# A graph attention layer on one core: VectorE's order of work at a change of super-row

## The reference

```python
h = relu(layernorm(x))                                   # 8192 x 256
Wh = h @ W_w + W_b
e = leaky_relu((Wh @ a1)[:, None] + (Wh @ a2)[None, :])  # 8192 x 8192
attention = softmax(where(adj > 0, e, -9e15), axis=1)
out = x + attention @ Wh
```

## Time and profile before

| | |
|---|---|
| time, median of 3 runs | 1593.36 us (1593.07 to 1595.46) |
| time of the profiled execution | 1592.53 us |
| its span, first to last instruction | 1590.7 us |
| TensorE busy | 1464.8 us (92%) |
| VectorE busy | 1421.9 us (89%) |
| ScalarE busy | 1116.6 us (70%) |
| GpSimd busy | 592.6 us (37%) |
| the 16 DMA engines, mean use in a super-row | 0.72 to 0.75 |

### The profile page before, as it was taken

How to read it: one execution, slowest core, us unless ns; L and a number is a source line. 1 busy time by engine, 2 the same in 40 slices (tenths; PEclk the granted TensorE clock), 3 DMA queues, 4 the chain that set the end, 5 groups by cost and what they waited for, 6 DMA issues and landing times.

```text
span 1590.7 us, 30593 instructions
## 1 busy us (share of the span) xinstructions
PE 1464.8 (92%) x12740; PEld 1266.0 (80%) x12740; DVE 1421.9 (89%) x1155; ACT 1116.6 (70%) x975; POOL 592.6 (37%) x1096
## 2 busy tenths in 40 slices
PE   3870999989999899999999999989999999989998
PEld 2750887768888788878888788878888888878887
DVE  4655999999999799979999799979999799979994
ACT  3655788868777687758776687758776677758771
POOL 0956333334444344333443344424443344424000
PEclk9995999999999999999999999999999999999999
DMA  9719766677777677776777677766777677767000
GB/s 193 79 10 132 55 43 46 48 94 67 54 52 64 91 52 52 67 95 46 53 53 70 83 56 51 65 92 48 53 54 75 80 51 55 51 87 53 2 1 28
DMA packets 170786, 99.36 MB, mean 62 GB/s; under 512 B 19472, under 2 KB 167568, under 8 KB 170640
## 3 DMA queue, kind: packets, MB, share of 16 engines
q0 software_dynamic: 147456, 67.17, 59.6%
q1 hardware_dynamic: 23184, 30.05, 7.0%
HBM read 290.06 MB, written 8.42 MB: 188 GB/s over the span
## 4 chain that ended last, share of the span: by engine, by line
PE 82%; DVE 11%; issue 3%; DMA 2%; ACT 1%; SPq 0%; DVEq 0%; POOL 0%; ACTq 0%; POOLq 0%
PE acc L594 77%; DVE work L503 4%; PE acc L570 3%; DVE work L496 3%; DVE X L509 1%; DMA work<-in_x 1%; PE acc L562 1%; DMA q_rows<-q_j 1%; DVE adj_cols L445 1%; PE acc L605 1%; ACT work L338 1%; DVE xr L396 1%; ACT work L323 1%; DMA work<-q_rows 0%; DVE xr L520 0%
## 5 line engine op out<-in xcount | busy, mean ns | idle before, releaser
L594 PE MATMUL acc<-X,work 128*128 128x257 f16 x12288 | 1387.9, 275 | 12.9 <-DVE work L503 12.9
L594 PEld LDWEIGHTS acc<-X,work 128*128 128x128 f16 x12288 | 1197.4, 98 | 195.3 <-DVE work L503 16.8
L251 POOL DMA_DIRECT2D adj_rows<-in_adj x1024 | 549.6, 545 | 819.6 <-DVE adj_cols L445 796.1
L338 ACT ACTIVATE work<-work 128x2048 f16<-128x2048 f32 x256 | 488.3, 1908 | 325.7 <-PE acc L594 276.7
L503 DVE SCALAR_TENSOR_TENSOR work<-work 128x2048 f16<-128x2048 f32 x256 | 584.8, 2284 | 64.3 <-ACT work L338 63.6
L496 DVE SCALAR_TENSOR_TENSOR work<-work,sigma,adj_cols 128x2048 f32<-128x2048 f32 x256 | 593.7, 2319 | 19.5 <-issue 16.3
L323 ACT ACTIVATE work<-work,r_j 128x1024 f32<-128x1024 f32 x256 | 278.4, 1135 | 24.9 <-DMA work<-q_rows 16.9
L323 ACT ACTIVATE work<-q_odd,r_j 128x1024 f32<-128x1024 f32 x256 | 278.9, 1136 | 12.1 <-DVE work L503 11.9
L445 DVE STREAM_TRANSPOSE adj_cols<-adj_rows 128x512 int32<-128x512 int32 x256 | 175.8, 697 | 0.0
L605 PE MATMUL acc<-mean_wh,tiny 128*128 128x257 f16 x64 | 19.4, 302 | 70.7 <-DVE work L503 58.9
L570 PE MATMUL acc<-q_odd,xr 128*128 128x258 f32 x256 | 69.1, 394 | 8.2 <-DVE X L414 8.2
(11 more groups left out here) (60 smaller groups left out, 53.7 us busy)
## 6 DMA issues: line engine op xcount, KB each, us to landing
adj_rows<-in_adj POOLq DMA_DIRECT2D x1024, 64.0 KB, 3.7
work<-in_x SPq DMA_DIRECT2D x16, 512.0 KB, 22.0
xr<-in_x SPq DMA_DIRECT2D x16, 512.0 KB, 6.1
out<-xr SPq DMA_DIRECT2D x16, 512.0 KB, 4.1
work<-q_rows SPq DMA_DIRECT2D x4, 512.0 KB, 5.7
q_odd<-q_rows SPq DMA_DIRECT2D x4, 512.0 KB, 5.5
q_odd<-in_L_gnn_W_w SPq DMA_DIRECT2D x2, 128.0 KB, 2.1
xr<-in_L_gnn_a SPq DMA_DIRECT2D x2, 128.0 KB, 5.8
```

Source lines behind the costliest of these rows:

```text
L251: pool.dma_start(rows8[QP * q:QP * (q + 1), n % R8], adj_v[s, m, k, q]).then_inc(s_rows[n % R8], 16)
L338: nc.scalar.mul(Et[:, at:at + 2, 0, :], Wt[:, i % RING], SCALE).then_inc(s_H, 1)
L594: return nc.tensor.matmul(acc[:, m, 0:F1], Et[:, 2 * (k % RING) + e, 1 if n == 2 else 0, m * P:(m + 1) * P], X16[:, 2 * k + e, 1 if n == 1 ...
```

## The change

At each of the 7 changes of super-row VectorE's first chunk is written out in another order. The weights of unit 3 move ahead of the first half of the reads, those of unit 4 between the halves, those of unit 5 behind the second half, ahead of `low` of unit 2. The weights of unit 6 move ahead of `turn(g, 3)` and `low` of unit 4. The other 25 chunks keep their order, and so does the loop on TensorE. On ScalarE `product(g, 5)` goes ahead of `high(g, 2)`. No instruction is added or taken away on any engine.

```diff
+            def between_rows(g):
+                product(g, 5)
+                high(g, 2)
...
+                    if g and g % NC == 0 and i == 1:
+                        between_rows(g)
+                    if g and g % NC == 0 and i in (1, 2):
+                        if i == 2:
+                            high(g, 3)
+                            product(g, 6)
+                        continue
...
+            def chunk_after_last(g):
+                weights(g, 1)
+                low(g, 0)
+                turn(g, 0)
+                weights(g, 2)
+                low(g, 1)
+                weights(g, 3)
+                turn(g, 1)
+                finish(g // NC - 1, 0)
+                weights(g, 4)
+                finish(g // NC - 1, 1)
+                weights(g, 5)
+                low(g, 2)
+                turn(g, 2)
+                low(g, 3)
+                weights(g, 6)
+                turn(g, 3)
+                low(g, 4)
+                turn(g, 4)
+                weights(g, 7)
+                low(g, 5)
+                turn(g, 5)
+                low(g, 6)
+                turn(g, 6)
+                turn(g, 7)
+                weights(g + 1, 0)
+                low(g, 7)
...
-                    if start and i == 2:
-                        finish(g // NC - 1, 0)
-                    if i + 1 < NI:
-                        weights(g, i + 1)
-                    elif g + 1 < NC * NS:
-                        weights(g + 1, 0)
-                    if start and i == 2:
-                        finish(g // NC - 1, 1)
-                    unit_low(g, i)
...
+                if g and g % NC == 0:
+                    chunk_after_last(g)
+                else:
+                    chunk(g)
```

More of the change, by code:

```diff
@@ L531, in turn, with chunk @@
                     transpose(g + 1, m)
+            def chunk(g):
+                for i in range(NI - 1):
+                    weights(g, i + 1)
+                    unit_low(g, i)
+                    turn(g, i)
+                turn(g, NI - 1)
+                if g + 1 < NC * NS:
+                    weights(g + 1, 0)
+                unit_low(g, NI - 1)
+            def chunk_after_last(g):
[23 more added lines that the diff above has]
+                turn(g, 7)
+                weights(g + 1, 0)
+                low(g, 7)
             weights(0, 0)
             for g in range(NC * NS):
-                start = g and g % NC == 0
-                for i in range(NI):
-                    if start and i == 2:
-                        finish(g // NC - 1, 0)
-                    if i + 1 < NI:
-                        weights(g, i + 1)
-                    elif g + 1 < NC * NS:
-                        weights(g + 1, 0)
-                    if start and i == 2:
-                        finish(g // NC - 1, 1)
-                    unit_low(g, i)
[L546 to L549, removed]
+                if g and g % NC == 0:
+                    chunk_after_last(g)
+                else:
+                    chunk(g)
             for half in range(2):
```

## The result

| | before | after |
|---|---|---|
| time, median | 1593.40 us (6 runs, 1592.85 to 1595.46) | 1587.38 us (6 runs, 1586.38 to 1588.15) |
| ratio to before, 95% interval | | 0.9956 [0.9945, 0.9967] |
| profiled execution | 1592.53 us, span 1590.7 | 1588.15 us, span 1586.3 |

The forecast was no change at 1594.0 us, with a range of 1590.8 to 1598. The measured gain of 0.44% is small, but clear of the noise and outside the range.

The account below looks back on a forecast made before the run. TensorE was taken as the bound, with only some 40 us at six jumps able to move. The profiled 1592.53 + 0.1 (first change) + 0.6 (transfers) = 1593.2, or 1594.0 us on the median's scale; range 1590.8 to 1598.

Parts of the forecast that it names:

- the 40 us at the six jumps: TensorE's six jumps back: 57.5 us, 40.2 above their work; only this can give anything or grow.
- the names in the waits: At L605 the profile names `low` as releaser; the forecast said TensorE cannot have waited for it, the gap being the jump.
- rival 3: At L605, TensorE really waits for unit 2's `low` in three gaps or all: 8 to 16 us slower; chance 0.04.
- The margins of VectorE, ScalarE and the banks: Behind a change, later reads, `low` parts and products still arrive in time, banks 7 and 10 us ahead: cost 0.
- More lead: Units 6 and 7 come 2.25 us sooner from VectorE, but TensorE isn't waiting for it: brings 0.
- VectorE's idle time ahead of `low(g, 4)`: VectorE's idle time before unit 4's `low` at the second change: 7.59 us before, forecast 6.9.
- The first change: Change without a jump: first bank told 0.7 us later, as L605 starts; cost 0 to 0.3 us, 0.1 taken.
- Transfers move as well.: Store and mask loads shift nearer TensorE's instruction fetch at the jumps: +0.1 us each, 0.6 in all.
- no order of VectorE shortens the gap: At the jumps TensorE waits for its instruction fetch, not VectorE, so reordering VectorE gains 0 there.
- The bounds: All six jumps as the shortest, 9.14 us, give -2.6 us; as the longest +2.5; with 1.5 us more each +8.8.
- Rival 2: At the jumps, the later store frees the fetch and the slow clock shrinks: -4.5 us, 1589; chance 0.09.
- The long transfer of 2.4 us: An instruction fetch in a crowd took 2.4 us against 0.97, so at most 1.5 us more per jump.

Follow-up runs that it names:

- experiment 7: The changed kernel with TensorE's super-rows 1 to 7 written out instead of looped, so that nothing jumps; 1554.3 us, ratio 0.9751 to before.
- experiment 6: The kernel before with freed mask loads and first store both held until all eight banks are read; 1574.22 us, ratio 0.988.
- experiment 8: The changed kernel with the freed mask loads held on GpSimd until all eight banks are read; 1577.38 us, ratio 0.9892 to before.
- experiment 2: The kernel before with only the transpose turn(g, 1) moved behind the first half of the reads; 1594.28 us, ratio 0.9999.
- experiment 3: The kernel before with the freed mask loads held by one GpSimd wait until all eight banks are read; 1581.89 us, ratio 0.992.
- experiment 1: The changed kernel with the transpose turn(g, 1) back ahead of weights(g, 3); 1586.65 us, ratio 0.9958 to before.
- experiment 5: The kernel before with the first store held on SyncE until all eight banks are read; 1587.8 us, ratio 0.9967.
- experiment 9: The kernel before with only weights(g, 3) moved ahead of the first half of the reads; 1586.99 us, ratio 0.9954.

## Why the prediction was wrong

- **That the 40 us at the six jumps are the only thing that can move: right.** 39.4 us went with the loop. That the names in the waits (a `low` before, a read after) are coincidences of time was right too, and rival 3 is dead: in the changed kernel unit 2's `low` starts at 528.64, when TensorE has been running again since 527.13.
- **The margins of VectorE, ScalarE and the banks: right.** No product waits for `low` behind a change. More lead brought nothing, as experiment 7 shows. VectorE's idle time ahead of `low(g, 4)` was 5.90 us; 6.9 was worked out for a jump that takes as long as before, and this one is 1.4 us shorter.
- **The first change: right in kind, 0.1 taken, 0.46 us of standstill and 0.6 in all measured.** The length of the read was right; the instant at which TensorE wanted the bank was not read finely enough.
- **The step that failed: "Transfers move as well."** I saw that the store and the mask loads would shift by about 2 us. Then I took for granted that closer to the page's transfer means more in its way, and wrote +0.1 us for each jump. In truth the pages of before were in the middle of the crowd already: in the 5 us at the third change, 97% of the engines' time was mask loads and store. Issuing the store 1.6 us before the end and not 3.4 let the second page land 0.9 us sooner (1.85, not 2.74), and with it the standstill ended 0.9 us sooner. The term is -8.3 us in this profile, not +0.6. With it falls the sentence that no order of VectorE shortens the gap: VectorE does not end the gap, but its order sets when the store is issued. The rows that the term rests on tell how long a page took; none tells what else the queues moved in those microseconds.
- **The bounds were no bounds.** The best of six, 9.14 us, was taken as the floor. But all six jumps had the same transfers at the same distance. Their scatter is what chance does with one arrangement, and says nothing of another. The lowest mean with the loop is 6.1 us (experiments 6 and 8). Rival 2 had the mechanism with the right sign, but 0.09 of chance and a price of -4.5 us, since it was made from the same scatter. A mechanism whose sign I could not read deserved both signs in the range.
- **A page's length misled.** The long transfer of 2.4 us was the first page. What counts is when the second has landed, and its delay is all ahead of its transfer: it starts 1.3 us after the end before and 1.0 us ahead of the end with both held, means of six, and takes no longer. A share of busy time doesn't show that.

## What to carry to other kernels

A jump on the busiest engine costs what its instruction pages take to arrive, and then some slow clock; look at what the DMA queues move in the 5 us before it, and delay by a wait on the issuing queue what is not urgent. Better still, write the loop out where that can be done: here it is worth 39 us, against 6 for the change and 20 for the best arrangement with the loop. When several events look alike in one trace, their scatter bounds noise, not the effect of an edit that shifts them all.

## What the runs showed of the hardware

- A standstill of 2.35 us stayed without a fall of the clock in the windows row shown for experiment 6, and one of 3.75 us before was followed by 1.2 GHz products for two banks (2.58 us for 12 instead of 1.33). The granted clock fell to 0.50 behind all six jumps before, behind five in the changed kernel, three with the loads held, four with the store held and none with both. The length of the standstill doesn't decide alone: it fell behind 2.24 us in experiment 8 and not behind 3.18 us in the changed kernel. From before to experiment 6 the standstill shrank by 1.89 us and the stretch to the third bank by 3.49, so a microsecond of standstill can cost nearly two (an estimate from the table).
- In experiments 2 and 3 the same four loads, issued 2.9 us later, gave nothing, and issued 7.9 us later, 12 us. The Trainium skill says that each DMA engine takes its queues in turn, a whole packet at a time (DMA: Bandwidth & Descriptors, Queues, rings and completion order). The trace agrees only in that a page starts late among other transfers, the second one by 2.3 us before against experiment 6; how long one turn is, no run here shows.
- Open: why issuing the store later helps while the loads stay. In experiment 1 the loads are issued when they were before, and the records of the store's packets lie almost where they lay before (half of them have started by 0.4 us behind the end, before by 0.6). In the changed kernel they start between 0.1 and 2.7 us behind it, still beside the second page. What differs in both is that the store is issued 1.6 us ahead of the end and not 3.4, so that the pages may be asked for before it. Which request stood first in which queue can't be read from the records.
- Open: why the set-up took 1 to 5.5 us longer in the other profiled executions than in that of before, and why the runs of experiments 1, 5 and 9 spread over 6 to 9 us where those of the changed kernel spread over 2. Experiment 8 has the stretch at the jumps of experiment 6 and a median 3 us above it, but with four runs each (1574.2 to 1577.5 and 1572.1 to 1578.1) the two are not told apart.
